# New orders, early transfers and six-slot list marks in the opening stage of an attention and mixture-of-experts kernel

## The reference

```python
x = L0_attn_x                                   # 2 x 1024 tokens of 512 values
xn = _layernorm(x, axis=-1)
x = x + attention(xn, ...) + ffn(xn, ...)       # 16 heads in 4 groups; experts below

def _route(xf, Wr, br):                         # E=32 experts, 8 groups of 4, K=6
    s = jax.nn.sigmoid(xf @ Wr.T + br)
    sg = s.reshape(T, G, E // G)
    group_w = jax.lax.top_k(sg, 2)[0].sum(-1)
    top_g = jax.lax.top_k(group_w, KG)[1]       # the best 4 groups
    ...
    idx = jax.lax.top_k(masked, K)[1]           # the best 6 experts of a token
    w = jnp.take_along_axis(s, idx, axis=1)
    w = w / (w.sum(-1, keepdims=True) + 1e-20)
    return (idx, w * SCALE)

h = jnp.square(jax.nn.relu(xf @ w1.T)) @ w2.T   # one expert; M=256
shared = jnp.square(jax.nn.relu(hidden_tensor @ Ws1.T)) @ Ws2.T   # 512 hidden units
```

## Time and profile before

| what | value |
|---|---|
| median of 3 runs | 1538.15 us (1534.75 to 1538.18) |
| the profiled execution: time, span | 1538.73 us, 1537.0 us |
| TensorE, VectorE, ScalarE, GpSimd busy | 99%, 74%, 55%, 19% of the span |
| mean granted TensorE clock | 0.995 of 2.4 GHz |
| opening stage, to the first expert matmul | 0 to 150.63 us |

### The profile page before, as it was taken

How to read it: one execution, slowest core, us unless ns; L and a number is a source line. 1 busy time by engine, 2 the same in 40 slices (tenths; PEclk the granted TensorE clock), 3 DMA queues, 4 the chain that set the end, 5 groups by cost and what they waited for, 6 DMA issues and landing times.

```text
span 1537.0 us, 31138 instructions
## 1 busy us (share of the span) xinstructions
PE 1514.3 (99%) x8548; PEld 1304.8 (85%) x8549; DVE 1134.0 (74%) x2586; ACT 839.0 (55%) x1753; POOL 296.0 (19%) x540
## 2 busy tenths in 40 slices
PE   8998999999999999999999999999999999999998
PEld 7886888889989878888888888888888888888886
DVE  6796566666665669949948967976985994994896
ACT  4655666666666735635635644554553563563553
POOL 0001444434444301012002102102101101200211
PEclk8999999999999999999999999999999999999999
DMA  7692677777776621102102112512210210210111
GB/s 276 261 396 89 198 245 234 230 245 224 243 247 218 225 76 55 56 15 81 34 27 75 34 34 81 192 61 76 68 41 28 71 52 20 75 34 27 55 42 55
DMA packets 64774, 184.34 MB, mean 120 GB/s; under 512 B 7136, under 2 KB 7264, under 8 KB 60000
## 3 DMA queue, kind: packets, MB, share of 16 engines
q1 hardware_dynamic: 39888, 112.56, 21.0%
q0 software_dynamic: 16640, 54.54, 13.1%
q10 hardware_dynamic: 8208, 16.78, 2.8%
HBM read 123.29 MB, written 60.56 MB: 120 GB/s over the span
## 4 chain that ended last, share of the span: by engine, by line
PE 96%; DVE 3%; issue 0%; ACT 0%; DMA 0%; DVEq 0%; ACTq 0%; POOLq 0%
PE bank L665 9%; PE bank L667 9%; PE bank L666 9%; PE bank L989 8%; PE ps_s L665 7%; PE ps_s L667 7%; PE ps_s L666 6%; PE ps_s L976 5%; PE ps_s L978 4%; PE ps_s L977 4%; PE ps_s L857 4%; PE ps_s L880 3%; PE ps_s L861 3%; PE ps_s L858 3%; PE ps_s L884 3%; PE ps_s L881 3%
## 5 line engine op out<-in xcount | busy, mean ns | idle before, releaser
L1294 ACT ACTIVATE probs<-probs,negmax 128x128 f32<-128x128 f32 (+7 forms) x256 | 197.5, 774 | 122.6 <-DVE negmax L1702 122.0
L1302 ACT ACTIVATE pT_hi<-bank 128x512 fp32r<-128x512 f32 x288 | 164.3, 594 | 143.6 <-PE bank L989 117.6
L1321 DVE TENSOR_TENSOR pT_lo<-bank,pT_hi 128x512 fp32r<-128x512 f32 x288 | 189.7, 684 | 41.0 <-ACT pT_hi L1302 40.1
L1702 DVE CUSTOM_DVE_ANT_0 probs<-ps_s,causal 128x128 f32<-128x128 f32 (+7 forms) x256 | 189.4, 753 | 17.2 <-PE ps_s L978 15.0
L427 POOL TENSOR_TENSOR settled<-ident 128x1 f32<-128x1 f32 x192 | 45.0, 234 | 789.0 <-DVE acc L1731 779.1
L989 PE MATMUL bank<-ident,probs 128*128 128x128 f32 x1152 | 157.0, 272 | 0.0
L989 PEld LDWEIGHTS bank<-ident,probs 128*128 128x128 f32 x1152 | 136.9, 141 | 19.9
L665 PE MATMUL ps_s<-xT_hi,wa_hi 128*128 128x512 f32 x384 | 152.7, 398 | 0.0
L667 PE MATMUL ps_s<-xT_hi,wa_lo 128*128 128x512 f32 x384 | 151.0, 393 | 0.0
L666 PE MATMUL ps_s<-xT_lo,wa_hi 128*128 128x512 f32 x384 | 150.2, 391 | 0.0
L1711 DVE TENSOR_SCALAR probs<-probs,rnorm 128x128 f32<-128x128 f32 (+7 forms) x256 | 133.4, 521 | 9.1
(11 more groups left out here) (197 smaller groups left out, 3601.3 us busy)
## 6 DMA issues: line engine op xcount, KB each, us to landing
eraw<-we SPq DMA_DIRECT2D x37, 1024.0 KB
expert_outputs<-ysb SPq DMA_DIRECT2D x111, 256.0 KB
araw<-wa SPq DMA_DIRECT2D x37, 512.0 KB, 4.3
expert_outputs<-comb ACTq DMA_DIRECT2D x1, 16384.0 KB, 48.9
normed_tokens<-xn SPq DMA_DIRECT2D x4, 1024.0 KB, 9.2
out<-acc SPq DMA_DIRECT2D x16, 256.0 KB
acc<-x SPq DMA_DIRECT2D x2, 1024.0 KB, 13.8
turned_tokens<-xT_hi SPq DMA_DIRECT2D x2, 1024.0 KB, 5.5
```

The lines of the kernel that those rows point to most:

```text
L1294: act.activation(pr, pr, ACT.Exp, bias=negmax[:, i % 2, a:a + 1], scale=-1.0, accum_out=rowsum[:, i % 2, a:a + 1]).then_inc(exp_ready, 1)
L1302: act.activation(pT_hi[:, blk % RING, :], ps_t[blk % 2][:, :], ACT.Copy).then_inc(pt_hi_ready, 1)
L1321: dve.tensor_tensor(out_, whole, upper.bitcast(F32), ALU.subtract).then_inc(signal, 1)
L1702: dve.tensor_tensor_reduce(halves(probs[:, i % 2, a, 0:keys]), ps_s[:, s:s + parts, 0:keys // parts], halves(causal[:, SQ - keys:]), -1.0, ...
```

## The change

Four edits are made, all in the opening stage.

1. The wait for `started` moves from the head of the four engines' queues to the place at which they first need it, and GpSimd makes its constants (`ones` first) ahead of the semaphore increments. SP can so issue the loads of x at once, and TensorE waits for fewer constants before `turn_up(0, 0)`.
2. The queues of TensorE, ScalarE and VectorE have new orders; `lower_unit`, `square_unit` and a new `upper_unit` stand for half a unit each, and `outputs` waits for each `h_lo` half by itself and not for all four of its product. `WARM` falls from 16 to 12, and the warming matmuls further on rise from 8 to 12.
3. The marks of all six slots are made in one comparison of 16-bit numbers. `tile_hot` becomes [128, 160, 6] with the slots innermost, and `row_hot` of even tiles [128, 128 x 6] likewise. `lanes` holds each place six times over.
4. The token's number is multiplied into `row_hot` and no more into `tile_hot`: on VectorE in an operation of its own, on ScalarE as the scale and bias of the Relu. TensorE then reads both operands of an even tile, and `tile_hot` of an odd one, with a step of six elements (12 bytes); `row_hot` of odd tiles stays contiguous.

```diff
-WARM = 16
+WARM = 12
...
-                row_hot = sb("row_hot", [P, 2, TOPK, P], F16, inner)
-                tile_hot = sb("tile_hot", [P, 2, TOPK, MAXT], F16, inner)
+                row_hot = sb("row_hot", [P, 2, TOPK * P], F16, inner)
+                tile_hot = sb("tile_hot", [P, 2, MAXT, TOPK], F16, inner)
...
+                lanes = sb("lanes", [P, MAXT, TOPK], F16, inner)
+                part_16 = sb("part_16", [P, 2, TILES, 8], F16, inner)
+                tok_neg = sb("tok_neg", [P, TILES], F32, inner)
...
+        def rows_marked(t):
+
+            return row_hot[:, t % 2, :].rearrange("p (k r) -> p k r" if t % 2 else "p (r k) -> p k r", k=TOPK)
...
         def _(sp):
-            sp.wait_ge(started, 4)
...
             load_part(4)
+            sp.wait_ge(started, 4)
...
         def _(pool):
+            pool.memset(ones[:, :].bitcast(F32), 1.0).then_inc(ones_ready, 1)
...
+            pool.tensor_copy(lanes[:, :, :], tok_idx[:, 0:MAXT].unsqueeze(2).to_broadcast([P, MAXT, TOPK])
+                             ).then_inc(consts_ready, 1)
+            pool.wait_ge(consts_ready, 7)
+            pool.tensor_scalar(tok_neg[:, :], tok_f[:, :], -1.0, None, ALU.mult).then_inc(consts_ready, 1)
+
             for s in start_at_one:
...
             def outputs(o, q):
-                    pe.wait_ge(hlo_ready, (o + 1) * NSH * KM)
...
+                for k in range(NSH * KM):
+                    u, m = divmod(k, KM)
+                    if q == 0:
+                        pe.wait_ge(hlo_ready, o * NSH * KM + k + 1)
...
                 for k in range(TOPK):
-                    mm = pe.matmul(ps_list, row_hot[:, t % 2, k, :], tile_hot[:, t % 2, k, :],
+                    mm = pe.matmul(ps_list, rows_marked(t)[:, k, :], tile_hot[:, t % 2, :, k],
...
             def mark_rows(t):            (ScalarE)
-                act.activation(row_hot[:, t % 2, :, :], away[:, :, :], ACT.Relu, bias=scan_ones[:, 0:1],
-                               scale=-1.0).then_inc(row_marked, 1)
+                act.activation(rows_marked(t), away[:, :, :], ACT.Relu, bias=tok_f[:, t:t + 1],
...
             def mark_rows(t):            (VectorE)
+                row_of, tile_of = (part_16[:, i, t, 0:TOPK].unsqueeze(1) for i in range(2))
                 if t % 2 == 0:
-                    for k in range(TOPK):
-                        dve.tensor_scalar(row_hot[:, t % 2, k, :], lane[:, 0:P], part_f[:, 0, t, k:k + 1], None, ALU.is_equal)
-                for k in range(TOPK):
-                    last = dve.tensor_scalar(tile_hot[:, t % 2, k, :], lane[:, :], part_f[:, 1, t, k:k + 1],
-                                             tok_f[:, t:t + 1], ALU.is_equal, ALU.mult)
+                    rows = row_hot[:, 0, :]
+                    dve.tensor_tensor(rows.rearrange("p (r k) -> p r k", k=TOPK), lanes[:, 0:P, :],
+                                      row_of.to_broadcast([P, P, TOPK]), ALU.is_equal).then_inc(row_same, 1)
+                last = dve.tensor_tensor(tile_hot[:, t % 2, :, :], lanes[:, :, :],
+                                         tile_of.to_broadcast([P, MAXT, TOPK]), ALU.is_equal)
+                if t % 2 == 0:
+                    dve.wait_ge(row_same, t // 2 + 1)
+                    last = dve.tensor_scalar(rows, rows, tok_f[:, t:t + 1], None, ALU.mult)
                 last.then_inc(hot_ready, 1)
```

More of the change, by code:

```diff
@@ L574, in _ @@
         def _(pool):
-            for s in start_at_one:
-                pool.sem_inc(s, 1)
-            for half in range(2):
-                pool.sem_inc(y_stored[half], 1)
-            pool.sem_inc(y_free, YB - 2)
-            pool.sem_inc(mx_ready, XG)
-            pool.sem_inc(xT_ok, 64)
-            pool.sem_inc(z_ok, 16 * NT)
-            pool.sem_inc(aw_hi, 3)
-            pool.sem_inc(aw_lo, 3)
-            pool.sem_inc(araw_in[0], 32)
-            pool.sem_inc(araw_in[1], 16)
-            pool.sem_inc(started, 4)
             pool.memset(ones[:, :].bitcast(F32), 1.0).then_inc(ones_ready, 1)
@@ L607, in _ @@
             pool.tensor_copy(tok_f[:, :], tok_i[:, :]).then_inc(consts_ready, 1)
+            pool.tensor_copy(lanes[:, :, :], tok_idx[:, 0:MAXT].unsqueeze(2).to_broadcast([P, MAXT, TOPK])
+                             ).then_inc(consts_ready, 1)
+            pool.wait_ge(consts_ready, 7)
+            pool.tensor_scalar(tok_neg[:, :], tok_f[:, :], -1.0, None, ALU.mult).then_inc(consts_ready, 1)
+            for s in start_at_one:
+                pool.sem_inc(s, 1)
+            for half in range(2):
+                pool.sem_inc(y_stored[half], 1)
+            pool.sem_inc(y_free, YB - 2)
+            pool.sem_inc(mx_ready, XG)
+            pool.sem_inc(xT_ok, 64)
+            pool.sem_inc(z_ok, 16 * NT)
+            pool.sem_inc(aw_hi, 3)
+            pool.sem_inc(aw_lo, 3)
+            pool.sem_inc(araw_in[0], 32)
+            pool.sem_inc(araw_in[1], 16)
+            pool.sem_inc(started, 4)
             pool.wait_ge(list_ready, 1)
@@ L696, in logits @@
                 pe.wait_ge(xf_ready, s * NT + t + 1)
+                if s == 0 and t == 0:
+                    pe.wait_ge(consts_in, 32)
                 if s and t == 0:
@@ L761, in _ @@
             turn_up(0, 0)
+            warm(2)
             turn_up(0, 1)
+            warm(2)
             logits(0, 0)
+            logits(0, 1)
+            turn_up(0, 2)
+            turn_up(0, 3)
             warm(2)
-            turn_up(0, 2)
-            logits(0, 1)
+            logits(0, 2)
+            logits(0, 3)
+            warm(4)
+            turn_up(0, 4)
             warm(2)
-            turn_up(0, 3)
-            logits(0, 2)
-            warm(2)
-            logits(0, 3)
-            warm(2)
-            hidden(0, 0)
-            hidden(0, 1)
-            turn_up(0, 4)
             turn_up(0, 5)
@@ L1016, in _ @@
         def _(act):
-            act.wait_ge(started, 4)
             act.wait_ge(pool_chain, 2)
@@ L1633, in lower_weights @@
                 subtract(lo_slot(slot)[:, w_piece(c)], eraw[:, slot % 2, w_piece(c)], hi_slot(slot)[:, w_piece(c)], ew_lo)
+            dve.wait_ge(started, 4)
             lower_weights(0, 0, slot_of(0))
+            lower_unit(6, 0)
+            lower_unit(6, 1)
+            add_output(2, 3)
+            lower_unit(7, 0)
+            lower_unit(7, 1)
             lower_weights(0, 1, slot_of(0))
```

299 lines of the change are left out of this document (165 added, 134 removed).

## The result

The changed kernel takes 1542.07 us (median of 8 runs, 1540.07 to 1543.38) where the kernel before, on the same chip, takes 1537.81 (1533.63 to 1540.21): a ratio of 1.003, with a 95% interval of 1.0018 to 1.0043. I had predicted 1528.0 and a range of 1522 to 1538: the change made the kernel slower by 4.3 us, and not faster. The profiled execution took 1543.19 us, its span is 1541.4.

A forecast was written before the change was run, and what follows sets the result against it. TensorE, busy 99% of the span, was taken as the bound. Start -2.4, warming +1.3, early waits -0.5, early clock -2.0, later waits -5.6 and later clock -1.5 sum to -10.7: 1538.7 becomes 1528.0 us, range 1522 to 1538.

The forecast's parts named there:

- Reading with a step: TensorE's list matmuls: reading operands with a step of 12 bytes costs nothing, a term of 0.
- my upper bound of 7.7 from the transposes: List matmuls: at the transposes' rate per column, 0.147 us instead of 0.067, 7.7 us over 96 matmuls.
- Rival 1: List matmuls: the stepped read costs the transposes' rate, leaving a gain of 3.0 us, 1535.7 us; chance 0.15.
- rival 2: List matmuls: the stepped read makes the kernel slower, 0.23 us each instead of 0.067, or 1548 us at 0.28; chance 0.06.
- The start: Kernel's opening: x load issued near 0.5 us, first transposes at 6.9 instead of 9.41; term -2.4 us.
- The later waits: TensorE's waits around the list: of 6.6 us, 1.0 is left for ScalarE; term -5.6 us.
- VectorE has it then: List's end: VectorE finishes the last h_lo unit by 4.9 us after the list, when outputs(3, 0) needs it.
- The experts and the attention keep their code: Behind the opening stage: code unchanged and waits few, so no term was taken there.
- The clock at the start: Early batch 0: warming matmuls give back 2 of some 5 us lost at half clock; bounds 0 and 5.
- -2.4 and +1.3: Opening: -2.4 us for the earlier x load, +1.3 us for four more warming matmuls behind the data.
- rival 3: VectorE's marks: the comparison doesn't go in twos, 4 us of the gain lost, 1532 us; chance 0.09.
- rival 4: Batch 0's new order starves TensorE: hidden(0, 0) waits 2 to 3 us, 5 us lost, 1533 to 1536; chance 0.12.

The follow-up runs named there:

- e3: The changed kernel with two slots innermost instead of six, so TensorE reads with a step of 4 bytes instead of 12: 1528.96 us, ratio 0.994.
- e7: The changed kernel with groups of 24 extra matmuls at its end, reading operands at various steps, to time the step by itself: a single execution, 1603.73 us.
- e6: e3 with lower_weights(0, 0) moved on VectorE from ahead of lower_unit(6, 0) to behind lower_unit(7, 1): 1525.41 us, ratio 0.9914.
- e11: e6 without the twelve warming matmuls behind the first transposes; the first twelve stay: 1531.05 us, ratio 0.9948.
- e8: The kernel before with edit 1 alone (waits for started moved, GpSimd's constants ahead of the increments): 1537.50 us, ratio 0.9989.
- e4: The changed kernel with six slots still marked in one comparison, but slots outermost, the row or tile repeated along the innermost axis: 1532.42 us, ratio 0.9955.
- e12: e6 with 110 instructions of waits on a set semaphore added to VectorE's queue, at its head and where it stands idle: 1521.70 us, ratio 0.9895.

## Why the prediction was wrong

**The step that failed is "Reading with a step ... I take nothing."** My reason was that "twice the bytes a column already cost nothing". That is true for 4 bytes a column, which e3 and e7 confirm, and it says nothing about 12. The term was 0 and measured 13.7 us; my upper bound of 7.7 from the transposes was too low as well. Rivals 1 and 2 had the mechanism and neither had the size. Rival 1 (chance 0.15) priced a list matmul at 0.147 us, rival 2 (0.06) at 0.23 and more. It came to 0.217 (0.28 is what a step of 16 bytes costs, e7). Put into my sum, 13.7 instead of 0 gives 1538.7 - 10.7 + 13.7 = 1541.7, beside a median of 1542.07 and 1543.19 for the profiled execution. That it fits so well is chance, since other terms were off both ways. In the profiled executions the wait for `h_lo` and its clock cost 5.0 us, the attention 3.6 and the dip near 55 us 1.7. The start was 4.6 us better than I forecast: `hidden(1, 0)` (33.56 before) begins at 25.40, where my terms gave 30.0. The later waits were 1.0 us better, all 6.6 us gone instead of 5.6. Some 3 us of gain between 25 us and the first expert matmul are in none of these terms, and no run takes them apart. Of the two rules that I quoted from the Trainium skill (SBUF — State Buffer, Door 1: The DMA port swizzle), the first, at least two accesses of a line, pointed the right way: at 12 bytes a line of 16 has 1.33 accesses. But a step of 8 bytes has two and took 0.143 us, twice the time of a step of 1, so its limit isn't borne out by e7. The second, 8 bf16 elements for free, would have made the time 1528, and e7 has such a step at 0.283 instead of 0.070 us.

**"VectorE has it then" failed.** I added the times of what VectorE had to do ahead of `outputs(3, 0)` and left out what its first item waits for. `lower_weights(0, 0)` needs a ScalarE copy, queued behind `h_hi` of unit 7, which needs `outputs(2, 3)`, and this I had myself moved behind the list. Its price is 3.25 us, and 1.7 of clock behind it (6 us at 0.72). e6 takes the wait away and gains 3.6 us in all.

**"The experts and the attention keep their code" was true and no reason.** TensorE's and VectorE's code there is the same, but VectorE's lies 110 instructions further up, and that costs 3.6 us: 2.3 more of waiting, and some 1.7 of clock by estimate (14 us at 0.88), a little more together than what is lost. The rows of before show no stall at this place.

**The clock at the start was mis-sized, in the other direction.** I took 2 of some 5 us; it was all 5: the clock is 1.00 from 14 to 24. The reason is the one I gave, the warming matmuls in the gaps (e11), and they are worth more than the earlier x, which alone brings 0.8 us because the clock falls that much sooner (e8). So -2.4 and +1.3 aren't terms of their own. What the warming matmuls are worth without the earlier x was not measured.

**What held.** The first transposes at 7.06 (said: 6.9). 1.94 us a pair for the marks (1.9), at the fast rate, against rival 3; e4 shows how near it was, since with the row number along the innermost axis a pair takes 3.34 us (105.25 to 108.59). The waits for the marks went, all 5.3 us. `hidden(0, 0)` begins at 19.8 us (21), with no wait there, against rival 4. The fetch stayed hidden. With the step at 4 bytes, the weights behind unit 7 and the jump where it was, e12 gains 16.5 us, more than my 10.7: the mechanisms of the gain were there, and the step alone took back 13 to 14 us (e3).

## What to carry to other kernels

When a layout is changed for the engine that writes, price the engine that reads, per column, from a measurement at that step: here a step of 4 bytes is free for the moving operand and one of 12 costs three times. When an operation is moved, ask of everything that is queued behind it what it waits for, not only how long it takes. When instructions are taken out ahead of a jump, look at the trace behind the jump, however far it is. Where executions of one kernel differ in their granted clock, compare those at the same clock before giving a change at the start its price.
